# The opening of a fused graph-layer kernel: weight loads behind x, transposes by token tile, first low half and the mask's empty planes on GpSimd

## The reference, cut to what matters

```python
xn = layernorm(x)
# graph attention, 16 heads of 64
q = xn @ wq.T + bq; k = xn @ wk.T + bk; v = xn @ wv.T + bv
q2 = q @ wiq.T + biq; k2 = k @ wik.T + bik; v2 = v @ wiv.T + biv
mask = full((384, 384), -inf)
mask[src, dst] = softplus(edge_type_weights)[edge_type - 1]      # 12288 edges
mask[i, i] = softplus(edge_type_weights)[3] where no edge wrote it
attn = softmax(q2 @ k2.T / 8 + mask);  gnn = (attn @ v2) @ wo.T + bo
# linear attention of the same xn, with its own weights mq, mk, mv, mo
mix = (phi(xn @ mq.T) @ (phi(k).T v) / denom) @ mo.T + bo        # phi = elu + 1
x = x + gnn + mix
# 4 of 32 experts for each token
x = x + experts(layernorm(x))
```

## Time and profile before

| | |
|---|---|
| median of 3 runs | 999.03 us (998.47 to 999.04) |
| the profiled execution's own time | 996.85 us |
| its span in the profile | 994.9 us |
| TensorE busy | 901.2 us, 91% of the span |
| VectorE, ScalarE, GpSimd busy | 678.9, 508.6, 330.3 us |
| mean granted clock of TensorE | 0.969 |

### The profile page before, as it was taken

The page is one execution under the profiler, slowest core; times in us unless marked ns, Lnnn a source line. Parts: engine busy times, 40 slices in busy tenths (PEclk is TensorE's granted clock), DMA queues, the critical chain, the costliest instruction groups (busy, mean ns, idle before and its releaser), DMA issues.

```text
span 994.9 us, 14101 instructions
## 1 busy us (share of the span) xinstructions
PE 901.2 (91%) x4447; PEld 739.3 (74%) x4447; DVE 678.9 (68%) x1128; ACT 508.6 (51%) x710; POOL 330.3 (33%) x294
## 2 busy tenths in 40 slices
PE   3889999999999999898954999999999999999993
PEld 3878889989989999445833777777777777777772
DVE  6776676633434544674675688888988888888883
ACT  3343322323323322674220587777777777877772
POOL 0613445544440000895001122343323333223331
PEclk9889999999999999999975999999999999999997
DMA  7433322233334333001662399999999999999951
GB/s 300 156 129 125 115 106 85 85 128 127 128 132 170 127 127 127 1 1 43 253 243 74 132 329 324 347 336 340 343 331 333 336 336 336 323 345 338 343 187 20
DMA packets 40454, 203.01 MB, mean 204 GB/s; under 512 B 12880, under 2 KB 13136, under 8 KB 18400
## 3 DMA queue, kind: packets, MB, share of 16 engines
q1 hardware_dynamic: 25632, 183.51, 50.1%
q0 software_dynamic: 13200, 15.03, 6.2%
q10 hardware_dynamic: 1584, 3.97, 1.0%
HBM read 203.33 MB, written 21.15 MB: 226 GB/s over the span
## 4 chain that ended last, share of the span: by engine, by line
PE 61%; DVE 16%; issue 9%; POOL 6%; ACT 4%; DMA 2%; ACTq 0%; DVEq 0%; POOLq 0%; SPq 0%
PE ps L1074 19%; PE ps L1076 18%; PE ps L1075 18%; POOL pr L375 6%; DVE wl L794 3%; ACT wh_x L618 3%; DVE xgTl L1029 3%; DVE wl_x L794 2%; DVE hTl L1035 2%; PE ps L1104 1%; PE ps L1191 1%; DMA acc<-in_x 1%; DVE etmp L1041 1%; PE ps L1114 1%; DVE ysb L1041 1%
## 5 line engine op out<-in xcount | busy, mean ns | idle before, releaser
L608 ACT ACTIVATE wh<-raw 128x1024 fp32r<-128x1024 f32 x88 | 93.2, 1061 | 251.6 <-PE ps L1076 240.7
L755 DVE TENSOR_TENSOR wl<-raw,wh 128x1024 fp32r<-128x1024 f32 x88 | 109.8, 1252 | 154.8 <-ACT wh L608 154.4
L525 POOL DMA_INDIRECT plane<-code,idx x96 | 100.5, 1047 | 119.4 <-DMA plane<-code,idx 81.4
L1074 PE MATMUL ps<-wh,xgTh 128*128 128x512 f32 x248 | 101.0, 407 | 20.1 <-DVE wl L794 20.1
L1074 PE MATMUL ps<-wh_x,hTh 128*128 128x512 f32 x248 | 105.8, 427 | 0.0
L794 DVE TENSOR_TENSOR wl_x<-raw_x,wh_x 128x1024 fp32r<-128x1024 f32 x64 | 76.7, 1222 | 34.4 <-ACT wh_x L618 34.4
L1076 PE MATMUL ps<-wh,xgTl 128*128 128x512 f32 x248 | 98.0, 395 | 0.0
L1075 PE MATMUL ps<-wl,xgTh 128*128 128x512 f32 x248 | 97.8, 395 | 0.0
L1076 PE MATMUL ps<-wh_x,hTl 128*128 128x512 f32 x248 | 97.7, 394 | 0.0
L1075 PE MATMUL ps<-wl_x,hTh 128*128 128x512 f32 x248 | 97.3, 392 | 0.0
L794 DVE TENSOR_TENSOR wl_x<-raw,wh_x 128x1024 fp32r<-128x1024 f32 x64 | 76.6, 1220 | 29.9 <-ACT wh_x L618 29.9
(11 more groups left out here) (218 smaller groups left out, 2050.7 us busy)
## 6 DMA issues: line engine op xcount, KB each, us to landing
raw<-in_keys SPq DMA_DIRECT2D x34, 1024.0 KB, 10.7
raw_x<-in_values SPq DMA_DIRECT2D x34, 1024.0 KB, 10.7
raw_x<-in_keys SPq DMA_DIRECT2D x30, 1024.0 KB, 11.2
raw<-in_values SPq DMA_DIRECT2D x30, 1024.0 KB, 12.0
raw<-in_w_v SPq DMA_DIRECT2D x8, 1024.0 KB, 4.8
raw<-in_w_q SPq DMA_DIRECT2D x8, 1024.0 KB, 4.8
raw<-in_w_k SPq DMA_DIRECT2D x8, 1024.0 KB, 4.7
raw<-in_w_mq SPq DMA_DIRECT2D x4, 1024.0 KB, 7.8
```

The source lines that it names most:

```text
L525: nc.gpsimd.indirect_dma_start(plane[m], bass.IndirectOffsetOnAxis(idx[:, g:g + 1].bitcast(U32), 0), code[:, g:g + 1], None, bounds_check= ...
L608: nc.scalar.activation(wh[:, s % SUB], raw[:, c % RAW, 2 * (s % 2):2 * (s % 2) + 2, :], ACT.Copy)\
L755: nc.vector.tensor_tensor(wl[:, s % SUB], raw[:, (s // 2) % RAW, 2 * (s % 2):2 * (s % 2) + 2, :], wh[:, s % SUB].bitcast(F32), ALU.subtrac ...
L1074: nc.tensor.matmul(o, ah, bh_, start=start, stop=False)
```

## The change

In words:

- SyncE no longer waits for `s_const`: the first four weight chunks, and the three rows behind them, are issued right behind x.
- ScalarE issues the identity's 128 columns first, then the edges and edge-type weights; then it waits until the last tile of x is in, and issues the rest of `c_all`, the biases and `sel`. TensorE's first wait is for the identity alone.
- TensorE transposes all eight chunks of a token tile before the next tile, into all eight banks. The loop of xT1 is skipped, and the wait for the constants stands behind the transposes.
- GpSimd, idle until then, fills `none`, makes the low half of sub 0 when ScalarE has made its high half (`s_hi` at 1), and writes `none` into both planes by six transfers. VectorE's `split` begins at sub 1; subs 1, 2 and 3 stand between the evacuations of xT1 and ahead of the edge work of mq0. ScalarE makes subs 2 and 3 inside xT1.
- At mq0 and mq1 the edge work on VectorE now stands ahead of `split(j["sub_end"] + LEAD)`, not behind it. `empty_planes` is gone; the diagonal goes into the first plane by three indirect transfers of GpSimd, from indices `diag` and the value `w4[:, 4, 3:4]`.

```diff
--- before.py
+++ after.py
@@ -139,8 +139,6 @@
         late = at("late", [P, NT, N], F32, F1 + 6 * KB)
         is_late = at("is_late", [P, N], F32, F1)
         none = at("none", [P, N], F32, A2 + 8 * KB)
-        diag = at("diag", [P, N], F32, A2 + 8 * KB + 1536)
-        is_diag = at("is_diag", [P, NT, N], F32, A2 + 11 * KB)
 
         pT = at("pT", [P, PTS, NT, N], F32, A1)
         sm = at("sm", [P, RING, N], F32, A0)
@@ -211,6 +209,7 @@
         mx = sb("mx", [P, 4, H * NT], F32)
         gcol = [sb(f"gcol{p}", [P, 1], I32) for p in range(2)]
         pcol = sb("pcol", [P, 1], I32)
+        diag = sb("diag", [P, NT], I32)
         slots = sb("slots", [P, 1], I32)
 
         ps = [ctx.enter_context(nc.psum_tensor(f"ps{b}", [P, 512], F32)) for b in range(8)]
@@ -233,7 +232,9 @@
         s_xn = sem("s_xn")
         s_spl = sem("s_spl")
         s_idx = sem("s_idx")
-        s_base = sem("s_base")
+        s_ident = sem("s_ident")
+        s_none = sem("s_none")
+        s_weight = sem("s_weight")
         s_init = sem("s_init")
         s_edge = [sem("s_edge0"), sem("s_edge1")]
         s_plane = sem("s_plane")
@@ -320,15 +321,6 @@
                 link(nc.vector.tensor_scalar(dup[:, :], typ, float(k), w4[:, 4, k:k + 1], ALU.is_equal, ALU.mult))
                 link(nc.vector.tensor_tensor(code[:, :], code[:, :], dup[:, :], ALU.add))
 
-        def empty_planes(link):
-
-            link(nc.vector.memset(none[:, :], NEG))
-            link(nc.vector.tensor_scalar(diag[:, :], cst["iota"][:, :], 0.0, w4[:, 4, 3:4], ALU.mult, ALU.add))
-            for t in range(NT):
-                link(nc.vector.tensor_copy(mask[:, t, :], none[:, :]))
-                link(nc.vector.tensor_scalar(is_diag[:, t, :], cst["iota"][:, :], cst["own"][:, t:t + 1], None, ALU.is_equal))
-                nc.vector.copy_predicated(mask[:, t, :], is_diag[:, t, :].bitcast(U32), diag[:, :]).then_inc(s_base, 1)
-
         def attention_dve(dve):
 
             def masked(u, n):
@@ -452,7 +444,6 @@
         def _(sp):
             for t in range(NT):
                 sp.dma_start(acc[:, t, :], x[t * P:(t + 1) * P, :]).then_inc(s_x[t], 16)
-            sp.wait_ge(s_const, 16 * N_CONST)
             for c in range(CHUNKS):
                 if c >= RAW:
                     sp.wait_ge(s_lo, 2 * (c - RAW + 1))
@@ -501,6 +492,13 @@
         @block.gpsimd
         def _(pool):
 
+            nc.gpsimd.memset(none[:, :], NEG).then_inc(s_none, 1)
+            pool.wait_ge(s_hi, 1)
+            nc.gpsimd.tensor_tensor(wl[:, 0], raw[:, 0, 0:2, :], wh[:, 0].bitcast(F32), ALU.subtract).then_inc(s_lo, 1)
+            pool.wait_ge(s_none, 1)
+            for m in range(2):
+                for t in range(NT):
+                    pool.dma_start(plane_rows[m][:, t, :], none[:, :]).then_inc(s_init, 16)
             pool.wait_ge(s_rows, 16 * N_ROWS)
             pool.wait_ge(s_xn, NT)
             for t in range(NT):
@@ -509,11 +507,12 @@
             for t in range(NT):
                 nc.gpsimd.tensor_tensor(acc[:, t, :], acc[:, t, :], mbo_b[:, :], ALU.add).then_inc(s_bias, 1)
 
-            pool.wait_ge(s_base, NT)
-            pool.dma_start(plane_rows[0], mask[:, :, :]).then_inc(s_init, 16)
-            for t in range(NT):
-                pool.dma_start(plane_rows[1][:, t, :], none[:, :]).then_inc(s_init, 16)
-            pool.wait_ge(s_init, 16 * (NT + 1))
+            pool.wait_ge(s_init, 16 * 2 * NT)
+            pool.wait_ge(s_weight, 1)
+            for t in range(NT):
+                nc.gpsimd.indirect_dma_start(plane[0], bass.IndirectOffsetOnAxis(diag[:, t:t + 1].bitcast(U32), 0), w4[:, 4, 3:4], None,
+                                             bounds_check=N * N - 1, oob_is_err=False).then_inc(s_init, 16)
+            pool.wait_ge(s_init, 16 * 3 * NT)
             for k in range(0, len(GROUPS), 2):
                 pool.wait_ge(s_idx, k + 2)
                 for q in range(GROUP):
@@ -584,11 +583,13 @@
 
         @block.scalar
         def _(act):
+            act.dma_start(call[:, 0:P], C["all"][:, 0:P]).then_inc(s_ident, 16)
             act.dma_start(ei[:, :, :], edges).then_inc(s_const, 16)
             act.dma_start(w4[:, 0, :], etw.to_broadcast([P, 4])).then_inc(s_const, 16)
+            act.wait_ge(s_x[NT - 1], 16)
+            act.dma_start(call[:, P:], C["all"][:, P:]).then_inc(s_const, 16)
             act.dma_start(col[:, :, :], cols).then_inc(s_const, 16)
             act.dma_start(sel[:, :, :], selT).then_inc(s_const, 16)
-            act.dma_start(call[:, :], C["all"]).then_inc(s_const, 16)
 
             done = [0]
             chain = [0]
@@ -646,12 +647,14 @@
                     pb = bank_of(j, b)
                     if b == 1 and split_early(name) and not name.startswith("xT"):
                         split(j["sub_end"] + LEAD + 1)
+                    if name == "xT1" and b in (0, 2):
+                        split(3 + b // 2)
                     base = j["base"]
                     if base in ("xT", "mT"):
                         bank_filled(act, j, b)
                         if name == "mT0" and b == 0:
                             act.wait_ge(s_bias, NT)
-                            act.wait_ge(s_init, 16 * (NT + 1))
+                            act.wait_ge(s_init, 16 * 3 * NT)
                         nc.scalar.activation((xnh if base == "xT" else mbh)[:, 4 * oh_ + b, :], pb[:, 0:N], ACT.Copy).then_inc(s_ahi, 1)
                     elif base in into:
                         bank_filled(act, j, b)
@@ -746,12 +749,14 @@
                 ins.then_inc(s_dch, 1)
                 dve.wait_ge(s_dch, chain[0])
 
-            done = [0]
+            done = [1]
 
             def split(upto):
 
                 for s in range(done[0], min(upto, SUBS)):
                     dve.wait_ge(s_hi, s + 1)
+                    if s == 1:
+                        dve.wait_ge(s_lo, 1)
                     nc.vector.tensor_tensor(wl[:, s % SUB], raw[:, (s // 2) % RAW, 2 * (s % 2):2 * (s % 2) + 2, :],
                                             wh[:, s % SUB].bitcast(F32), ALU.subtract).then_inc(s_lo, 1)
                 done[0] = max(done[0], min(upto, SUBS))
@@ -800,11 +805,10 @@
                 if name == "att":
                     attention_dve(dve)
                     continue
-                if not name.startswith("xT"):
-                    split(j["sub_end"] + LEAD)
                 half = int(name[-1]) if name[-1].isdigit() else 0
                 base = j["base"]
                 if name == "mq0":
+                    split(4)
 
                     dve.wait_ge(s_const, 16 * N_CONST)
                     link(nc.vector.tensor_copy(ef[:, 0:3, :], ei[:, :, :]))
@@ -819,12 +823,17 @@
                     link(nc.vector.memset(mv[:, :, :, P], 1.0))
                 if name == "mq1":
                     dve.wait_ge(s_ra, 1)
-                    link(nc.vector.scalar_tensor_tensor(w4[:, 4, :], w4[:, 0, :], 0.0, w4[:, 3, :], ALU.max, ALU.add))
+                    link(nc.vector.tensor_scalar(diag[:, :], cst["own"][:, 0:NT], float(N + 1), None, ALU.mult))
+                    nc.vector.scalar_tensor_tensor(w4[:, 4, :], w4[:, 0, :], 0.0, w4[:, 3, :], ALU.max, ALU.add).then_inc(s_weight, 1)
+                    dve.wait_ge(s_weight, 1)
                     edge_values(link)
-                    empty_planes(link)
+                if not name.startswith("xT"):
+                    split(j["sub_end"] + LEAD)
                 for b in range(j["banks"]):
-                    if b == 1 and (name.startswith("xT") or split_early(name)):
-                        split(half if name.startswith("xT") else j["sub_end"] + LEAD + 1)
+                    if name == "xT1" and b in (0, 2):
+                        split(2 + b // 2)
+                    if b == 1 and split_early(name) and not name.startswith("xT"):
+                        split(j["sub_end"] + LEAD + 1)
                     pb = ps[4 * j["set"] + b]
                     if name != "lin":
                         bank_filled(dve, j, b)
@@ -1080,9 +1089,21 @@
 
             needs = {"mo": "mT", "v2": "v", "q2": "q", "k2": "k", "mq": "xT"}
             end = {n: jobs[n]["first"] + jobs[n]["banks"] for n in order}
-            pe.wait_ge(s_const, 16 * N_CONST)
+            pe.wait_ge(s_ident, 16)
             for name in order:
                 j = jobs[name]
+                if name == "xT1":
+                    continue
+                if name == "xT0":
+
+                    for t in range(NT):
+                        pe.wait_ge(s_xn, t + 1)
+                        for o in range(DC):
+                            last = nc.tensor.transpose(ps[o][:, t * P:(t + 1) * P], xn[:, t, o * P:(o + 1) * P], ident)
+                            if t == NT - 1:
+                                last.then_inc(s_bank, 1)
+                    pe.wait_ge(s_const, 16 * N_CONST)
+                    continue
                 if name == "att":
                     attention_pe(pe)
```

(10 more changed lines are left out.)

## The result

The changed kernel took 991.79 us (median of 4 runs, 991.59 to 993.11), the kernel before 998.84 (4 runs, 998.47 to 999.04): a ratio of 0.9933, 95% interval 0.9915 to 0.995, or 7.05 us less (5.0 to 8.5 by the interval). The forecast was 995.0 (986 to 997.8), 4.0 us less. The two profiled executions differ by 5.26 us (996.85 and 991.59), their spans by 5.2; where the other 2 us come from is taken up further down.

What follows compares the result with a forecast made beforehand. TensorE, busy for 91% of the span, was taken as the bound, so only its opening losses could be won. Later mq1 (-1.2), slow clock (-1.6) and second gap (+6.8) gave 4.0 us: 999.03 to 995.0, range 986 to 997.8.

Steps and rivals of the forecast that it cites:

- The second gap: Before mk0: 4.3 us of wait and 2.5 of slow clock saved, together 6.8; up to 0.5 might come off.
- The collision in the opening: GpSimd's low half of sub 0 stops VectorE's normalisation chain for 2.4 us; first tile at 17.0, first product at 22.7.
- two inputs: Opening: two-input VectorE steps and GpSimd operations shut each other out for the whole instruction; hence 2.4 us taken.
- Turns with the adds set mq1: Before mq1: VectorE's edge steps alternate with GpSimd's bias adds at 2.4 us each, delaying mq1 to 47.4.
- S: Start of mq1 on TensorE: forecast 47.4, 1.2 us later than the old 46.2.
- The slow clock at mq1: After TensorE's longer idling, 5.6 to 6 us at low clock fall on mq1: loss 1.6 us.
- The sum: Whole kernel: -1.2 - 1.6 + 6.8 = 4.0 us gained, median 995.0.
- Escape of the edge steps: Rival before mq1: edge steps all finish before the adds start; 12.5 to 14.9 us gained, 984 to 986.5; 17%.

Runs made afterwards that it cites:

- Late adds: Changed kernel with GpSimd's six bias adds begun only after nine low halves, behind VectorE's edge work: 985.62 us, ratio 0.9872 to the kernel before.
- planes only: Kernel before with planes taken off VectorE; GpSimd writes them behind its adds and scatters the diagonal: 991.58 us against 996.93.

## Why the prediction was right, point by point

- *The second gap is the gain.* Forecast: mk0 without its wait and at full clock, 6.8 less at most 0.5. Measured: 6.5 us between the starts of dup1 and dup2, in the changed kernel and in the one with this part alone. That one gains 5.35 by the medians, and its mk0 starts 3.3 us earlier and at full clock. Shown.
- *The collision in the opening.* Forecast: GpSimd's half near 12.7 for 2.4 us, a small step stretched to about 2 us, first product 22.7. Measured: 12.51, 2.34, 2.25, 22.42. Moving the half behind the normalisation brought the first product 1.75 us forward. Shown. The reason that the prediction gave, two inputs, isn't what the trace tested: the step that stood there has one, and was held all the same; had it slipped through, the TENSOR_TENSOR behind it would by its place in the chain (near 12.8) still have met the half, so the size hardly hung on it. The Trainium skill's rule ("SBUF — State Buffer", section "Who interferes with whom") gave the direction. That section also names tensor_scalar among the forms that can contend, when their operands meet certain conditions, and the trace agrees for this one (2.25 us in place of 0.17).
- *Turns with the adds set mq1.* Forecast S = 47.4, measured 46.77; adds from 27.3, measured 26.95; edge steps at 2.4, measured 2.26 to 2.50. Moving the adds removed the wait. Shown. Off by 0.6: the last add ended at 42.3 and not 42.8, as the adds began 0.35 us earlier and the turns were a little shorter, and the three low halves behind took 3.42 us where I had 3.5.
- *The slow clock at mq1.* Forecast 5.6 to 6 us, measured 4.3. mq1 took 18.97 us to dup1's start, 18.03 before: 0.94 lost in place of 1.6.
- *The sum.* By the traces, 5.0 at dup2 for a forecast of 4.0: 0.6 more from S, 0.65 from the clock, and 0.2 less in the second gap (6.55 for 6.8). The step that was mis-sized is the slow stretch after the longer wait, with S next.
- *The rest of the 7.05.* The profiled pair differs by 5.3. The profiled execution of before was faster by 1.6 us or more than its other runs (998.47 to 999.04), at a mean granted clock of 0.969; in the later runs executions of before with 0.972 took 996.0 to 997.3 us and those with 0.967 took 997.6 to 999.9. The changed kernel's four have 0.971 to 0.974. The router products' 5.6 us (500.1 to 505.7) against 7.0 show one place within the profiled pair. The forecast carried the profiled pair's difference over to the medians, and the median gained 2 us more than the pair: that share of the 7.05 was no part of the forecast. Why more executions of before have the lower clock wasn't tested and stays open.
- *Escape of the edge steps.* It didn't happen, by 3.4 us (cast at 30.37, first add at 26.95). Late adds made it happen, and mk0 then came 7.4 us earlier: the size that I had given it, 12.5 to 14.9 under before, is what that kernel measured (13.2).

The best version, late adds with the low half on VectorE, planes behind it and constants at dup0, took 982.73 us against 998.29: 9 us below the changed kernel (8.6 by the ratios), of which the late adds alone give 6.

## What to carry to other kernels

Work moved to an idle engine isn't free if it can hold up another engine's operations, as GpSimd's did VectorE's here (2.25 us for a step of 0.17): look at what the other engine does in those microseconds, and above all whether it runs a chain of many short steps, each of which can be held for a whole long operation of the other. Before an opening is polished, find the latest queue that everything passes (here GpSimd's adds before mq1): moving it was worth 6 us, and what comes out behind it of a gain ahead of it (1.7 of 2.0 us in one kernel) or of a loss (none of 1.0 in another) has to be read from the trace. And an early wait may be keeping other things apart, here plane writes from x: take the wait away and look at what starts early.

## What was not expected

- A VectorE step on three columns was held for 2.25 us, one on four columns for 2.25 (0.16 when free). On 96 columns it was 2.23 to 2.50: in these traces the price of a turn is that of the GpSimd operation, not of the small one.
- Six writes of 192 KB issued at 1.47 us made x land 1.8 us later.
- The length of the slow stretch after a wait isn't fixed: 4.3 us behind 5.5 us of idling, and about 6.4 us behind 3.1. Nor is its place: behind the same 3.1 us, dup0 ran at a clock of 0.50 in the kernel before and at 1.00 in the kernel with planes only (1.93 us for 3.65), where the slow stretch came in mq1.
